# 48-expert stage of an eight-layer kernel: expert outputs added to token rows by accumulating indirect DMAs into two sums in DRAM, in place of 0/1 matmuls

## The reference, cut to what matters

```python
NUM_KEPT, TOP_K, HIDDEN, INTER, CAP = 48, 8, 256, 96, 96
pos = jnp.sum(jnp.cumsum(oh, axis=0) * oh, axis=-1) - 1
valid = pos < CAP
xb = jnp.zeros((E, CAP + 1, H)).at[flat_e, pos_c].set(x[tok])[:, :CAP]
g, u = jnp.split(jnp.einsum('ech,eoh->eco', xb, gate_up_proj), 2, axis=-1)
out = jnp.einsum('eci,ehi->ech', jax.nn.silu(g) * u, down_proj)
y = out[flat_e, jnp.minimum(pos_c, CAP - 1)]
final = jnp.zeros_like(x).at[tok].add(y * w[:, None])
```

## Time and profile before

| | |
|---|---|
| median of 3 runs | 1376.85 us (1371.93 to 1379.61) |
| the profiled execution's own time | 1375.91 us |
| its span in the trace | 1374.1 us |
| mean granted clock of PE in it | 0.746 of full |
| PE, DVE, ACT, POOL busy | 79%, 79%, 55%, 54% of the span |
| the stage of the 48 experts | about 593 to 749 us of the span |

### The profile page before, as it was taken

One profiled execution on the slowest core, in us unless ns is written; L12 is line 12 of the kernel. 1 busy time (PEld: TensorE's weight loads), 2 busy tenths in 40 slices (PEclk: granted clock), 3 DMA queues, 4 the chain that ended last, 5 costly groups with the idle time before them and its releaser, 6 DMA issues.

```text
span 1374.1 us, 30731 instructions
## 1 busy us (share of the span) xinstructions
PE 1084.8 (79%) x11431; PEld 711.6 (52%) x11431; DVE 1079.4 (79%) x2440; ACT 761.6 (55%) x1506; POOL 744.1 (54%) x831
## 2 busy tenths in 40 slices
PE   5830599981699899659998558878888899996998
PEld 3520499860333322537876435555556655653565
DVE  7889377657999999688885798888888576669784
ACT  4428243340598898424443368888889543334432
POOL 5787677755101410023343379888888838672361
PEclk9955799995655555779998855555555599997999
DMA  9941365542399898328762259899798511110000
GB/s 358 405 205 80 95 128 129 131 139 73 51 180 173 182 182 177 89 69 215 213 196 80 52 102 149 153 145 153 144 145 144 97 43 46 58 47 23 24 24 31
DMA packets 401923, 176.33 MB, mean 128 GB/s; under 512 B 364912, under 2 KB 383600, under 8 KB 399344
## 3 DMA queue, kind: packets, MB, share of 16 engines
q1 hardware_dynamic: 395680, 158.80, 51.4%
q0 software_dynamic: 4800, 13.11, 3.1%
q10 hardware_dynamic: 1296, 2.48, 0.6%
HBM read 63.04 MB, written 22.81 MB: 62 GB/s over the span
## 4 chain that ended last, share of the span: by engine, by line
PE 37%; DVE 30%; POOL 12%; DMA 7%; ACT 6%; issue 6%; SPq 1%; POOLq 0%; ACTq 0%; DVEq 0%
PE s_all L1081 22%; DVE small L2563 7%; PE bank L1081 4%; POOL c_hi L987 3%; POOL ffbuf L855 2%; POOL c_lo L987 2%; PE s_all L1491 2%; PE s_all L1088 2%; POOL c_hi L985 2%; PE s_all L1299 2%; PE bank L1299 1%; ACT arena L1741 1%; DVE small L2566 1%; DMA xt_hi<-c_lo 1%; DVE ffbuf L2405 1%
## 5 line engine op out<-in xcount | busy, mean ns | idle before, releaser
L1081 PE MATMUL s_all<-xt_hi,arena 128*96 128x128 f16 (+2 forms) x1448 | 201.4, 276 | 11.7 <-DVE xt_lo L2069 5.4
L1888 ACT ACTIVATE arena<-s_all,small 128x1024 int16<-128x1024 f32 x128 | 154.1, 1204 | 19.4 <-DVE small L2566 9.5
L2563 DVE TENSOR_REDUCE small<-s_all 128x1 f32<-128x1024 f32 x128 | 155.5, 1215 | 8.0 <-PE s_all L1491 7.9
L1081 PEld LDWEIGHTS s_all<-xt_hi,arena 128*128 128x128 f16 (+1 forms) x1448 | 104.7, 106 | 62.5 <-DVE xt_lo L2069 6.1
L1491 PE MATMUL s_all<-arena 32*128 32x512 f16 x256 | 130.1, 610 | 8.8 <-ACT arena L1888 4.5
L1088 PE MATMUL s_all<-zeros 128*128 128x512 f16 x124 | 41.4, 502 | 110.8 <-DVE moments L2054 58.5
L880 POOL DMA_INDIRECT arena<-rows,slot_misc x24 | 28.0, 1168 | 178.5 <-DVE slot_misc L2214 174.8
L775 POOL TENSOR_TENSOR arena<-arena,ws_col 128x768 f16<-128x768 f32 (+1 forms) x36 | 51.0, 1417 | 134.0 <-PE bank L1081 120.1
L1556 PE MATMUL s_all<-arena 32*128 32x256 f16 x512 | 91.8, 399 | 36.0 <-DVE small L2643 32.7
L1081 PEld LDWEIGHTS bank<-arena 128*128 128x128 f16 x2088 | 100.4, 106 | 37.4 <-issue 14.7
L1081 PE MATMUL bank<-arena 128*128 128x9 f16 (+1 forms) x2088 | 114.5, 191 | 6.2 <-DVE arena L2411 3.3
(11 more groups left out here) (403 smaller groups left out, 2825.5 us busy)
## 6 DMA issues: line engine op xcount, KB each, us to landing
arena<-in_w_pairs SPq DMA_DIRECT2D x16, 1024.0 KB, 10.1
arena<-in_w_experts SPq DMA_DIRECT2D x48, 320.0 KB, 4.4
arena<-in_w_blocks SPq DMA_DIRECT2D x36, 384.0 KB, 3.0
slots<-zeros SPq DMA_DIRECT2D x1, 8064.0 KB, 31.1
outs<-xn SPq DMA_DIRECT2D x63, 128.0 KB, 2.0
arena<-in_w_attn SPq DMA_DIRECT2D x4, 512.0 KB, 10.1
arena<-arena SPq DMA_TRANSPOSE x122, 2.8
x<-in_x_in SPq DMA_DIRECT2D x2, 512.0 KB, 4.5
```

Source lines behind the costliest of these rows:

```text
L1081: m = nc.tensor.matmul(outp, lhs, rhs, start=(first and n == 0), stop=(last and n == len(steps) - 1), skip_group_check=True)
L1888: nc.scalar.activation(p2[n % P2_BUFS], s2[n % S2_BUFS], ACT.Exp, bias=small[:, 1, s * L2_UNITS + v:s * L2_UNITS + v + 1], scale=scale_g[s ...
L2563: nc.vector.tensor_reduce(small[:, 0, c:c + 1], s2[(g * L2_UNITS + v) % S2_BUFS], AX.X, ALU.max).then_inc(G[2, "chain"], 1)
```

## The change

Slots are no longer packed in chunks of 128: each expert's 96 slots are handled by themselves. The gathers become four of 96 rows per quad, and so do the transposes. The turned 0/1 matrices, the combine matmuls and the sums in PSUM are gone. `down(q)` writes each expert into a bank of its own, ACT alone evicts it as float32 (`y3`, multiplied by the weight), and POOL adds its 96 rows to DRAM by an indirect DMA with `compute_op=add`. There are two such sums of 1152 rows of 1 KB (`sums3`), for even and odd experts. Unused slots read zero rows and add to rows past the 1024 tokens. Each add waits for the one two before it to have landed. The sums are cleared by two DMAs in sublayer 1, after its first five `tile_turn`s. After the last quad SP waits for all adds, loads both sums (four DMAs of 512 KB) and DVE adds them to x. Index buffers rise from 2 to 6, buffers of gathered rows from 6 of 128 to 8 of 96 rows.

```diff
-ROW_BUFS = 6
+ROW_BUFS = 2 * QUAD
+IDX_BUFS = 6
+        rows = nc.dram_tensor("rows", (T + CAP, 2 * D), F16, kind="Internal").ap()
+        sums3 = [nc.dram_tensor(f"sums3_{a}", (T + P, D), F32, kind="Internal").ap() for a in range(2)]
# SP
+            def clear_sums3():
+                for a in range(2):
+                    sp.dma_start(sums3[a].rearrange("(n p) d -> p n d", p=P),
+                                 zeros16[:, :].bitcast(F32).unsqueeze(1).broadcast_to([P, NT + 1, D])
+                                 ).then_inc(s_table, 16)
+            def add_sums3():
+                for a in range(2):
+                    sp.wait_ge(moved[a], MOVED1 + 16 * KEPT // 2)
+                for h, done in enumerate((s_map, s_table)):
+                    for a in range(2):
+                        sp.dma_start(add3[a][:, 4 * h:4 * h + 4, :],
+                                     sums3[a][4 * h * P:4 * (h + 1) * P, :].rearrange("(t p) d -> p t d", p=P)
+                                     ).then_inc(done, 16)
             for n in range(XT1_BUFS):
                 tile_turn(n)
+            clear_sums3()
...
             sp.wait_ge(we_lo, UNITS1 + KEPT - QUAD)
+            add_sums3()
# POOL
-                for q in range(QUADS):
+                def gather(q):
                     pool.wait_ge(s3_idx, q + 1)
...
+                    if q > 1:
+                        pool.wait_ge(s3_xe, 16 * QUAD * (q - 1))
+                    for e in range(QUAD):
                         nc.gpsimd.indirect_dma_start(
+                            out=x_rows[(q * QUAD + e) % ROW_BUFS][0:CAP, :], out_offset=None, in_=rows,
+                            in_offset=bass.IndirectOffsetOnAxis(ap=slot_idx[0:CAP, q % IDX_BUFS, e:e + 1], axis=0)
                         ).then_inc(ex_rows, 16)
+                def scatter_add(q):
+                    for e in range(QUAD):
+                        n = QUAD * q + e
+                        pool.wait_ge(s3_yh, n + 1)
+                        if n > 1:
+                            pool.wait_ge(moved[n % 2], MOVED1 + 16 * (n // 2))
+                        nc.gpsimd.indirect_dma_start(
+                            out=sums3[n % 2],
+                            out_offset=bass.IndirectOffsetOnAxis(ap=slot_idx[0:CAP, q % IDX_BUFS, e:e + 1], axis=0),
+                            in_=y3[q % 2][0:CAP, e, :], in_offset=None, compute_op=ALU.add).then_inc(moved[n % 2], 16)
+                for q in range(3):
+                    gather(q)
+                for q in range(QUADS):
+                    scatter_add(q)
+                    if q + 3 < QUADS:
+                        gather(q + 3)
...
-                pool.wait_ge(s3_c, QUADS + 1)
+                pool.wait_ge(s3_c, 2)
# PE
                 def down(q):
                     pe.wait_ge(ex_hl, TILES1 + q + 1)
+                    for j in range(QUAD):
+                        if q:
+                            pe.wait_ge(s3_yh, QUAD * (q - 1) + j + 1)
...
+                        mm3(bank[4 + j][0:CAP, 0:D], [pair]).then_inc(ex_y, 1)
-                def combine(q):
-                    for c in range(CHUNKS):
-                        chunk_ready(q, c)
-                        for i in range(NT):
-                            m = add_tile(q, c, i)
# ACT
+                    if q > 1:
+                        for a in range(2):
+                            act.wait_ge(moved[a], MOVED1 + 16 * QUAD * (q - 1) // 2)
+                    for e in range(QUAD):
+                        act.wait_ge(ex_y, TILES1 + QUAD * q + e + 1)
+                        nc.scalar.activation(y3[q % 2][0:CAP, e, :], bank[4 + e][0:CAP, 0:D], ACT.Copy,
+                                             scale=w_slot[0:CAP, q % 4, e:e + 1]).then_inc(s3_yh, 1)
# DVE
-                    if q:
-                        hot_turned(q)
-                    for c in range(CHUNKS):
-                        dve.wait_ge(s3_yh, CHUNKS * q + c + 1)
-                        nc.vector.scalar_tensor_tensor(out=y16[q % 2][:, 1, c, :],
...
+                for h, (done, before) in enumerate(((s_map, 5), (s_table, 6))):
+                    dve.wait_ge(done, 16 * (before + 2))
+                    for a in range(2):
+                        xh = x[:, 4 * h:4 * h + 4, :]
+                        m = nc.vector.scalar_tensor_tensor(out=xh, in0=add3[a][:, 4 * h:4 * h + 4, :], scalar=g3[:, 0:1],
+                                                           in1=xh, op0=ALU.mult, op1=ALU.add)
...
                     measure(4, 4 * h, 4 * h + 4)
```

More of the change, by code:

```diff
@@ L533, in build @@
         e1_sums = sem("e1_sums")
-        e1_got = [sem(f"e1_got{j}") for j in range(2)]
+        moved = [sem(f"moved{j}") for j in range(2)]
         e1_add = sem("e1_add")
@@ L1297, in add_tile @@
-                def add_tile(q, c, i):
-                    for a in range(2):
-                        m = nc.tensor.matmul(bank[4 + i // 2][:, (i % 2) * D:(i % 2 + 1) * D],
-                                             hot_t[q % 2][:, c, i * P:(i + 1) * P], y16[q % 2][:, a, c, :],
-                                             start=False, stop=False, skip_group_check=True)
-                    return m
-                def chunk_ready(q, c):
-                    pe.wait_ge(ex_out, TILES1 + CHUNKS * q + c + 1)
-                    pe.wait_ge(s3_hot_t, CHUNKS * q + c + 1)
@@ L2224, in hot_turned, with slot_values @@
[L2224 to L2231 removed]
+                def slot_values(q, b):
+                    return bank[b][0:CAP, 3 * QUAD * (q % 4):3 * QUAD * (q % 4 + 1)].rearrange("p (e a) -> p e a", a=3)
@@ new lines, in slot_rows @@
+                def slot_rows(q, b):
+                    dve.wait_ge(s3_slot, q + 1 if q < 3 else q + 2)
+                    if q >= IDX_BUFS:
+                        for a in range(2):
+                            dve.wait_ge(moved[a], MOVED1 + 16 * QUAD * (q - IDX_BUFS + 1) // 2)
+                    tokens = slot_values(q, b)[:, :, 2]
+                    link(nc.vector.tensor_scalar(unused, tokens, 0.0, slot_misc[0:CAP, 53:54], ALU.is_equal, ALU.mult))
+                    nc.vector.scalar_tensor_tensor(out=slot_idx[0:CAP, q % IDX_BUFS, :], in0=tokens, scalar=-1.0, in1=unused,
+                                                   op0=ALU.add, op1=ALU.add).then_inc(s3_idx, 1)
@@ L2233, in weights_low, with slot_weights @@
+                def slot_weights(q, b):
+                    dve.wait_ge(s3_slot, 4 if q < 2 else max(q, 3) + 2)
+                    nc.vector.tensor_reduce(w_slot[0:CAP, q % 4, :], slot_values(q, b)[:, :, 0:2], AX.X, ALU.add
+                                            ).then_inc(s3_ws, 1)
                 def weights_low(q):
```

232 lines of the change are left out of this document (77 added, 155 removed).

## The result

The changed kernel takes **1443.61 us** (median of 4 runs, 1434.62 to 1448.74) against 1374.39 of the kernel before on the same chip (1368.69 to 1379.61): ratio 1.0498, 95% interval 1.0465 to 1.0531. The direction was right; the time is 39 us above the forecast and 4 us outside the range. The profiled execution took 1448.74 us.

A forecast was written before the change was run, and what follows sets the result against it. POOL's queue was to hold the stage at 12.2 us a quad: 23.1 for the stage, 1.5 for a cold sublayer 4 and 4 for the clearing, 28.6 on 1375.9, gave 1404.5, with the median 1405 us; range 1373 to 1440.

The forecast's parts named there:

- Added on POOL, the main term: Mid-stage POOL queue: four gathers and four adds a quad instead of three issues, 12.2 us a quad against 10.07 before.
- Eight issues with their gaps: POOL's queue, per quad: eight indirect DMAs at 1.07 us, 1.37 with the gap, 11.0 us in all.
- Wait for the landing: POOL's queue: each add waits for the add two before, landing 3.9 us after issue; 1.2 us of wait a quad.
- It does not bind: Round from a gather over transposes, matmuls and eviction to that quad's add: needs some 25 us, has three quads' time.
- Rival 3: Issues of 96 rows cost 0.8 us, the period falls to about 9.6 us: 1382 us; chance 0.17.
- the faster case: POOL's period drops to 8.5 us and PE keeps 2.4 GHz, so relief of PE and DVE comes through: 1366; chance 0.10.
- The start: Start of the stage: four transposes instead of three before the first gate_up move it by 1.3 us.
- The clearing: Sublayer 1: two clearing DMAs of 1152 KB delay the sixth tile's turn and stall full PE, +4 us (0 to 4.9).
- The end: After the last adds: landing at 759.8, loads of the sums, DVE's additions and measures, both halves ending at 772.1.
- a cold sublayer 4: Sublayer 4 starts with PE cold after some 20 us idle: +1.5 us, bounds 0 and 5.
- Rival 4: Adds slow in the DMA engines, landing 7 to 8 us after issue, period 15.8 us: 1441 us; chance 0.13.
- far above 1.2 us (then the wait is not the landing but the issue itself): Changed profile, POOL: an add's issue that long was listed as a sign that the prediction is wrong.

The follow-up runs named there:

- e12: e3 plus TensorE multiplying zeros where it would wait, ahead of gate_up and down: 1426.87 us, against 1427.03 of e3.
- e3: Changed kernel with DVE waiting for its own previous operation between the eight operations of its burst: 1427.03 us, against 1443.61.
- e4: Changed kernel with compute_op=add left out of the 48 adds, so rows overwrite the sums: 1434.92 us, against 1443.61.
- e13: Changed kernel without the 48 adds and the waits for them, and with the gaps of e3 in DVE's bursts: 1406.37 us.
- e16: e13 (no adds, gaps in DVE's bursts) plus TensorE multiplying zeros where it would wait: 1405.88 us, against 1406.37 of e13.
- e15: e3 with the small slot matmuls loading 128 columns of weights instead of 96: 1425.17 us, against 1427.03 of e3.
- e1: Changed kernel with the two clearing DMAs moved behind SP's first four expert loads: 1445.74 us, against 1443.61.
- e10: e3 with the two clearing DMAs moved just ahead of the writing of the rows on SP's queue: 1427.3 us, against 1427.03 of e3.
- e8: Changed kernel with the 0/1 matrices not built from quad 3 on, leaving bursts of four low weight halves: 1434.52 us, against 1443.61.

## Why the prediction was wrong

**The direction, and the bound, were right**: POOL's queue holds the stage, PE's lower clock (0.59 over 640 to 800 us) costs nothing there (e12), and relief of PE and DVE brought nothing.

**The turn of POOL, forecast 12.2, measured 16.1** (stated bounds 8.5 and 14.5), is the step that failed, in "Added on POOL, the main term". Its nine turns came to 144.7 us and not 109.8: 35 of the 44 us by which the profiled execution (1448.7) missed 1404.5. By its terms:

- *Eight issues with their gaps, forecast 11.0.* In e3, free of long issues, the adds average 1.55 us (74.3 us for 48) and the gathers about 1.0:

```profile
L893 POOL DMA_INDIRECT arena<-rows,slot_misc x24 | 24.7, 1031 | 126.1 <-DVE slot_misc L2210 119.4
...
L904 POOL DMA_INDIRECT sums<-arena,slot_misc x48 | 74.3, 1548 | 34.7 <-DMA sums<-arena,slot_misc 20.8
```

  In its nine turns they come to 12.6 with the gaps, so +1.6. The forecast priced an add's issue like a gather's, and took 1.21 for the dearest that the rows bear out. It costs 1.41 alone, 0.49 of that for accumulating (e4).
- *Wait for the landing, forecast 1.2.* The adds land 3.6 us after their issue began at the median of the changed kernel's (3.33 for the one at 705.89); forecast 3.9. The waits are 1.4 us a turn, and 1.7 in e3, part of it for evictions. Right within half a microsecond. The 2.2 us that the prediction read from the Trainium skill's "DMA: Bandwidth & Descriptors", on the anatomy of one DMA, were too low.
- *Shut out by DVE's bursts, forecast nothing.* 16.08 - 14.24 = 1.8 us a turn (15.31 - 13.66 = 1.65 by the silus), 17 us in the time. The forecast raised the price of an issue for running beside DVE, from rows whose issues were 0.96 and 1.21; that one can take 6.1 was in no row of the kernel before.

A turn is longer than a quad by the silus (15.31, 13.66), because the first two of the eleven distances hang on gathers that no add stands ahead of (12.4 and 12.7 us in the changed kernel).

The rest of the miss: the first add starts 11 us later than laid out (the start, the third gathers at 630.8 instead of 623 with the clearing counted, and one of them shut out), and the end is 5 us longer; what follows the moments is 6.6 us shorter than forecast.

**"It does not bind", of the round from a gather on, was wrong.** Without adds a quad is 12.22 us, 1.84 more than before (e13). So even a free add would have left the stage 11 x 1.84 = 20 us longer. The round counted was the one to that quad's add; the one that holds the stage without adds runs from a gather over four transposes (8.5 us to their landing) and PE to the slots, whose numbers a later gather waits for (e13, e16). Rival 3 and the faster case were thereby excluded; the forecast gave them 0.27.

**The start** was forecast 1.3 us later, for the fourth transpose. It is 5.4 later, of which 2.7 against 0.8 us for each of two slots is the largest piece: "32 matmuls, 1.0" held for 128 columns of weights (1.06 in e15), not for 96.

**The clearing**, forecast +4: the sixth tile waited 3.37 us, as laid out, and by the medians about 3 us arrive at the stage. But moving it away gains nothing that can be measured in the whole (e1, e10).

**The end**, from the changed kernel's trace, last add to moments:

```profile
807.20 1.41 POOL L904 DMA_INDIRECT sums<-arena,slot_misc  x1 [0.75 <-DMA sums<-arena,slot_misc]
...
810.62 2.03 SPq L698 DMA_DIRECT2D arena<-sums  x4
...
815.84 3.09 DVE L2275 SCALAR_TENSOR_TENSOR x<-arena,slot_misc,x 128x1024 f32<-128x1024 f32 x2 [16.74 <-DMA arena<-sums]
818.96 1.41 DVE L2039 BATCH_NORM_STATS2 stats<-x 128x6 f32<-128x256 f32 x4
820.28 5.21 DVE L2275 SCALAR_TENSOR_TENSOR x<-arena,slot_misc,x 128x1024 f32<-128x1024 f32 x2
...
826.97 0.64 DVE L2045 BATCH_NORM_AGGREGATE moments<-stats 128x2 f32<-128x6 f32 x8
```

Loads issued to moments is 16.4 us, forecast 12.3 (759.8 to 772.1): the four additions into x took 8.3 us and not 4.9, one of them 3.91. POOL's helper for sublayer 4 (L992 to L1006, 812 to 824 us) now ran beside them; that it is the cause fits, but no run separates it. POOL's memsets ran while SP's loads were under way. The 1.5 us for a cold sublayer 4, for which no row stood, did not show; the rest of the program was 5 us shorter. In the other changed kernels that rest is 619.5 to 625.6 us, so it may be scatter.

**The rivals.** Rival 4 named almost this time (1441) by a wrong mechanism: adds landing after 7 to 8 us. They land in about half that, and the DMA share was 0.66 over POOL's nine turns, against 0.77 from 640 to 730 us in the kernel before. That the time came within 3 us of it is luck. Of the signs listed, an issue "far above 1.2 us (then the wait is not the landing but the issue itself)" was the one that came true.

## What to carry to other kernels

An indirect DMA is work for POOL: before moving anything onto its queue, multiply the issues by a price read in the same form (accumulating or not) beside the same DVE work, and ask how long DVE runs there without a pause; where POOL is the bound, waits put into DVE's bursts can gain time (here 17 us). And leave out, in thought, the operation that seems to be the cost: here the stage without a single add was still slower than the kernel before, because a lap of gather, transposes and products then held it. Time freed on the busy engines is worth nothing where a queue on another engine takes their place.

## What the runs showed of the hardware

- An unbroken row of DVE operations on SBUF held up an indirect DMA's issue until the row ended: 5.7 us instead of 0.95 beside 4.9 us of DVE, 3.85 beside 3.0 (e8). Such a gather or plain scatter ends 0.8 us after the row, an add 1.3. It came about at six of nine bursts of the same form, and not at a row of 6 us in the kernel before; what decides that was not found.
- An issue hardly depends on its rows: 0.92 to 0.96 us for 96, where 128 took 0.95 and 0.96. Accumulating adds 0.49 us to it.
- Weights of 96 columns make a small matmul 85 ns long at a clock of 0.50, those of 128 columns 33 ns (e15).
- Two DMAs of 1152 KB of zeros drove the DMA share of a stretch of 10 us to 1.01, and PE waited 3.4 us for the transpose queued behind them (2.8 to 3.9 over 13 kernels); started beside other gathers (e1), one of these began 2.8 us late.
